# Attention loop reordered, masks by row groups, maxima split on GpSimd, setup by quads

## The reference

```python
x = x + tanh(g_xattn[0]) * L0_xattn(layernorm(x), ctx)       # 16 heads of 8, biases; context reshaped per head
x = x + tanh(g_ffn[0])   * L0_ffn(layernorm(x))              # ternary weights, quantized activations, gelu
x = x + tanh(g_xattn[1]) * L1_xattn(layernorm(x), ctx)       # one head of 128
x = x + tanh(g_ffn[1])   * L1_ffn(layernorm(x))              # as F0, gated
x = x + tanh(g_xattn[2]) * L2_xattn(layernorm(x), ctx)       # 16 query heads, one key and value head
x = x + tanh(g_ffn[2])   * L2_ffn(layernorm(x))              # switch: each row to 1 of 8 experts
x = x + tanh(g_xattn[3]) * L3_xattn(layernorm(x), ctx, mask) # 16 heads, causal, masked query rows
x = x + tanh(g_ffn[3])   * L3_ffn(layernorm(x))              # 128->512, 9 butterfly stages, gelu, 9 stages, 512->128
```

## Time and profile before

| | |
|---|---|
| median of 3 runs | 1479.29 us (1462.97 to 1483.99) |
| the profiled execution | 1479.73 us, span 1477.7 us, mean granted clock of TensorE 0.834 |
| busy PE, PEld | 1070.0 us (72%), 585.5 us (40%) |
| busy DVE, ACT, POOL | 930.5 us (63%), 683.8 us (46%), 271.2 us (18%) |
| attention of L0, first to last masked maxima operand | 104.0 to 328.7 us |
| attention of L2, the same | 618.1 to 857.8 us |
| end of routing, then the expert slots | 857.8 to 917.5, to 1028.4 us |
| attention of L3, the same | 1104.5 to 1385.5 us |

### The profile page before, as it was taken

How to read it: one execution, slowest core, us unless ns; L and a number is a source line. 1 busy time by engine, 2 the same in 40 slices (tenths; PEclk the granted TensorE clock), 3 DMA queues, 4 the chain that set the end, 5 groups by cost and what they waited for, 6 DMA issues and landing times.

```text
span 1477.7 us, 27813 instructions
## 1 busy us (share of the span) xinstructions
PE 1070.0 (72%) x8534; PEld 585.5 (40%) x8534; DVE 930.5 (63%) x2571; ACT 683.8 (46%) x1465; POOL 271.2 (18%) x398
## 2 busy tenths in 40 slices
PE   0848777775667466688988873988057888888889
PEld 0623334332345233234444441665012333333389
DVE  3824777764989899367756633777644555555444
ACT  0213555543865465457655531444023544544356
POOL 1220000000000000001222234799497000000000
PEclk9955999995669676599978865999557999999989
DMA  8270554435999100000000001222321000000001
GB/s 196 85 65 6 41 44 34 34 29 143 173 159 147 57 1 1 0 2 2 5 12 8 8 8 36 82 76 71 88 72 58 1 2 1 2 2 1 1 22 36
DMA packets 285143, 66.91 MB, mean 45 GB/s; under 512 B 206113, under 2 KB 277857, under 8 KB 285026
## 3 DMA queue, kind: packets, MB, share of 16 engines
q1 hardware_dynamic: 271968, 48.40, 22.7%
q0 software_dynamic: 4896, 14.18, 2.8%
q10 hardware_dynamic: 8162, 2.80, 0.8%
HBM read 34.80 MB, written 30.56 MB: 44 GB/s over the span
## 4 chain that ended last, share of the span: by engine, by line
PE 46%; DVE 29%; issue 13%; POOL 4%; ACT 3%; DMA 3%; ACTq 2%; DVEq 2%; another core or an unknown queue 0%; SPq 0%; POOLq 0%
PE bank L960 15%; PE bank L987 5%; DVE nmax L1371 4%; PE bank L963 3%; PE bank L953 3%; PE bank L1033 2%; PE bank L956 2%; DVE small L1545 2%; PE bank L1245 2%; PE bank L1253 2%; PE bank L971 2%; DVE o_inv L1453 2%; PE bank L1022 2%; PE bank L1072 1%; DVE q_one L1537 1%
## 5 line engine op out<-in xcount | busy, mean ns | idle before, releaser
L1371 DVE TENSOR_REDUCE nmax<-bank 128x8 f32<-128x1024 f32 x192 | 235.1, 1225 | 259.9 <-PE bank L963 254.8
L685 ACT ACTIVATE probs_space<-bank 128x1024 f32<-128x1024 f32 x192 | 196.4, 1023 | 337.7 <-PE bank L971 335.3
L960 PE MATMUL bank<-q_one,k_all 32*128 32x512 f32 x768 | 243.2, 705 | 19.0 <-DVE nmax L1371 10.6
L963 PE MATMUL bank<-k_one,q_all 32*128 32x512 f32 x768 | 248.9, 725 | 5.2 <-ACT k_one L693 3.4
L987 PE MATMUL bank<-probs_space,vals 128*32 128x128 f32 x3072 | 135.4, 298 | 0.0
L987 PEld LDWEIGHTS bank<-probs_space,vals 128*32 128x32 f32 x3072 | 78.0, 116 | 137.9 <-issue 136.9
L558 POOL TENSOR_TENSOR var_b<-stats 128x4 f32<-128x4 f32 x8 | 1.6, 203 | 706.9 <-DVE stats L1282 706.9
L960 PEld LDWEIGHTS bank<-q_one,k_all 32*128 32x128 f32 x768 | 66.6, 199 | 73.2 <-issue 72.2
L971 PE MATMUL bank<-nmax_one,ones_bf 12*128 12x512 bf16 x384 | 84.5, 412 | 0.0
L1412 DVE TENSOR_TENSOR nmax_one<-bank,max_row 128x512 bf16<-128x512 bf16 x96 | 66.3, 691 | 26.9 <-PE bank L1022 26.6
L1022 PE MATMUL bank<-ident_bf,nmax_parts 128*128 128x128 bf16 x96 | 22.7, 236 | 77.6 <-DVE nmax_parts L1399 74.4
(11 more groups left out here) (271 smaller groups left out, 2353.4 us busy)
## 6 DMA issues: line engine op xcount, KB each, us to landing
expert_rows<-zeros SPq DMA_DIRECT2D x8, 2128.5 KB, 35.0
late<-in_L_ffn_up_weights_dram POOLq DMA_DIRECT2D x9, 512.0 KB
late<-_L_ffn_down_weights_dram POOLq DMA_DIRECT2D x9, 512.0 KB
q_one<-expert_rows SPq DMA_DIRECT2D x40, 64.5 KB
x<-in_x_dram SPq DMA_DIRECT2D x4, 512.0 KB, 13.6
...
```

The source lines that it names most:

```text
L685: act.activation(probs[:, 2 * g:2 * g + 2, :, :].rearrange("k g i q -> k (g i q)"), bank_pair[1][:, :, :].rearrange("k g f -> k (g f)"), A ...
L960: pe.matmul(bank[2 + s], group(k_all, u, 2 * g + s), group(q_one, u, 2 * g + s), start=not masked, stop=False)
L963: m = pe.matmul(bank[s], group(q_all, v, 2 * f + s), group(k_one, v, 2 * f + s), start=not masked, stop=True)
L1371: dve.tensor_reduce(nmax[:, u % 2, 0, :].rearrange("q (g i) -> q g i", i=HG)[:, 2 * g:2 * g + 2, :], bank_pair[0][:, :, :].rearrange("q g ...
```

## The change

- **Attention order.** TensorE starts an iteration with the pair and the values product; the transposes of the output and of the parts follow; the output product moves behind the second pair. The wait for the masked maxima operand (`t_nm`) moves from the front of a pair to right before its matmuls against ones. VectorE does the maxima first, then the operand of line 1412.
- **Split.** In L0 and L3 the split runs on GpSimd (`split_maxima`), in L2 it stays on VectorE, interleaved with reciprocal and output. Query copies 0 and 1 go to ScalarE in L0 and L3.
- **Masks.** Per pair sixteen matmuls of 32 rows and 128 columns, each in the row group whose scores it precedes, from tables of 32-row blocks (`future_rep`, `past_rep`, `keep_rep`, `ident_blocks_bf`), which VectorE builds between F2 and L3.
- **Setup.** x and context are loaded in pieces of 1, 2, 2 and 3 quads; the norm is made per piece on GpSimd (`norm_of`). `project(c)` handles a quad: ScalarE normalizes, TensorE transposes and projects, VectorE adds biases, SyncE stores it. It is called in iterations t = c - 14 of L0, so all eight come before the pairs of quad 0; quad 0 is reloaded at t = -13. Loads of the other weights move to SyncE's queue (`later_weights()`, at t = 1).
- **Routing.** The ring of normalized rows is written by GpSimd; distances shrink, and GpSimd is one quad behind, not two.
- **F2 and butterfly.** The contraction matrix is loaded after L2; it, the bias and the mask are transposed at the front of F2. All butterfly steps move to `beside_last_attention()`: per tile of L3 a split and then three steps (four from the 55th step on).
- Several semaphores are shared under new names.

```diff
+SPLIT_BY_POOL = ("L0", "L3")
+STATS_BEFORE = {"L2": 5, "L3": 7}
+NORMS = {"L2": 4, "L3": 5}
...
+R_XT, R_HOT, R_RANK, R_ROW = 7, 10, 11, 12
...
+PROJECT = 14
+CHUNKS = ((0, 1), (1, 3), (3, 5), (5, 8))
...
+    def chunk_load(c):
+        first, last = CHUNKS[c]
+        b, columns = slice(QT * first, QT * last), slice(QT * first * P, QT * last * P)
+        sp.dma_start(x[:, columns].rearrange("p (b d) -> p b d", d=P),
+                     A["x"][b].rearrange(tok)).then_inc(S(f"chunk_in{c}"), 16)
+        if c == 0:
+            layer0_weight(2, "L0_xattn_wv")
+            layer0_weight(1, "L0_xattn_wk")
+            layer0_weight(3, "L0_xattn_wo")
+        sp.dma_start(context[:, columns].rearrange("p (b d) -> p b d", d=P),
+                     A["ctx_1024"][b].rearrange(tok)).then_inc(S(f"ctx_in_o_back{c}"), 16)
+    layer0_weight(0, "L0_xattn_wq")
     for c in range(4):
+        chunk_load(c)
...
+    def later_weights():
+        for n in range(2):
+            sp.wait_ge(S(f"q_out_slot_in{n}"), 16 * NQ // 2)
...
+            c = t + PROJECT
+            if live(c, NQ):
+                rows = slice(QT * c, QT * c + QT)
+                for n, (scratch, stage, name) in enumerate(((q_scratch, stage_q, "q_out_slot_in"),
+                                                            (v_scratch, stage_v, "st_v"))):
+                    sp.wait_ge(S("a_qv"), 2 * c + n + 1)
+                    past(sp, f"{name}{c % 2}", 16 * (c // 2))
+                    sp.dma_start(scratch[rows].rearrange("u h (r c) d -> (h r) u (c d)", r=8),
+                                 stage[:, rows, :]).then_inc(S(f"{name}{c % 2}"), 16)
+            if t == 1:
+                later_weights()
...
+    def norm_of(first, n):
+        at, mean2, diff2 = slice(first, first + n), twice_mean[:, 0:n], spread[:, 0:n]
+        link(pool.tensor_tensor(var_b[:, at], stats[:, at, 1], stats[:, at, 4], ALU.subtract), False)
+        link(pool.tensor_tensor(var_a[:, at], stats[:, at, 2], stats[:, at, 5], ALU.add), False)
...
+        link(pool.tensor_tensor(shift[:, at], mean2, var_a[:, at], ALU.mult))
+    for first, last in CHUNKS:
+        pool.wait_ge(S("stats"), QT * last)
+        norm_of(QT * first, QT * (last - first))
+        pool.sem_inc(S("a_norm"), 1)
...
+    def split_maxima(first, v):
+        done = 4 * (first + v)
+        whole, left = (nmax[:, v % 2, i, :].rearrange("q (g i) -> q g i", i=HG) for i in range(2))
+        rows = nmax_parts[:, v % 2, :].rearrange("q (g n i) -> q g n i", g=NG, i=HG)
+        pool.wait_ge(S("t_mx"), 2 * (first + v + 1))
+        past(pool, "t_mt", first + v - 1)
+        pool.tensor_copy(rows[:, :, 0, :], whole).then_inc(S("t_na"), 1)
...
+    def beside_last_attention():
         pool.wait_ge(S("w_f3"), 16 * 2)
         pool.wait_ge(S("con_T"), 1)
-        pool.wait_ge(S("wq_ready"), 5)
+        pool.wait_ge(S("B_res"), NT)
+        butterfly_weights(0)
+        butterfly_weights(1)
+        k = 0
+        for v in range(NT):
+            split_maxima(2 * NT, v)
+            for _ in range(3 if k < 6 * STAGES else 4):
+                if k < 12 * STAGES:
+                    butterfly_step(k)
+                    k += 1
+    for v in range(NT):
+        split_maxima(0, v)
...
+            norm_of(QT * c, QT)
+            past(pool, f"scattered_{c % 4}", 16 * QT * (c // 4))
+            for w in range(QT * c, QT * c + QT):
+                pool.tensor_scalar(ring[:, w % ROUTE_RING, 0:P], tile_of(x, w), rstd[:, w:w + 1], shift[:, w:w + 1],
+                                   ALU.mult, ALU.add).then_inc(S("R_xn"), 1)
...
-        for c in range(NQ + 2):
+        for c in range(NQ + 1):
             if c < NQ:
                 norm_of_quad(c)
-            if c >= 2:
-                rows_of_quad(c - 2)
-                scatter(c - 2)
+            if c >= 1:
+                rows_of_quad(c - 1)
+                scatter(c - 1)
...
-            if "F3" in phases and s_no == 0:
-                butterfly_weights(0)
-                butterfly_weights(1)
-            if "F3" in phases and s_no >= 2:
-                butterfly_step(s_no - 2)
-    if "F3" in phases:
-        pool.wait_ge(S("B_res"), NT)
-        for k in range(NS - 2, 12 * STAGES):
-            butterfly_step(k)
+    beside_last_attention()
...
         def pair_of_scores(u, g, v, f):
             if live(u):
-                pe.wait_ge(S("t_nm"), tiles + u + 1)
-                pe.wait_ge(S("t_q1"), 2 * (quads + u // QT + 1))
-                pe.wait_ge(S("t_q1_dve"), 2 * (quads + u // QT + 1))
+                pe.wait_ge(S("t_q23"), 2 * (quads + u // QT + 1))
+                pe.wait_ge(S("t_q01"), 2 * (quads + u // QT + 1))
                 past(pe, "t_ex", 2 * (tiles + u) + g)
             if live(v):
+                pe.wait_ge(S("t_qa"), quads + v // QT + 1)
                 pe.wait_ge(S("t_k1"), HG * (quads + v // QT + 1))
                 past(pe, "t_mx", 2 * (tiles + v) + (1 - f))
             if masked:
-                for s in range(2):
-                    if live(u):
-                        pe.matmul(bank[2 + s], future_bf[:, :], over_blocks(keep_diag[:, u, :], HG),
-                                  start=True, stop=False)
-                    if live(v):
-                        pe.matmul(bank[s], keep_diag[:, v, :], over_blocks(future_bf[:, :], HG),
-                                  start=True, stop=False)
+                for b in range(HG):
+                    at = slice(HR * b, HR * b + HR)
+                    for s in range(2):
+                        if live(u):
+                            rows = slice(HR * (2 * g + s), HR * (2 * g + s) + HR)
+                            pe.matmul(bank[2 + s].rearrange("k (i q) -> k i q", i=HG)[:, :, at],
+                                      future_rep[rows, b, :], over_blocks(keep_rep[rows, u, b, :], HG),
+                                      start=b == 0, stop=False)
+                        if live(v):
+                            rows = slice(HR * (2 * f + s), HR * (2 * f + s) + HR)
+                            pe.matmul(bank[s].rearrange("q (i k) -> q i k", i=HG)[:, :, at],
+                                      past_rep[rows, b, :], over_blocks(ident_blocks_bf[rows, :], HG),
+                                      start=b == 0, stop=False)
...
             if live(u):
+                pe.wait_ge(S("t_nm"), tiles + u + 1)
...
+            u, w = t - lag, t - R_XT
+            routed = layer == "L2" and live(w)
+            if not own and t == 0:
+                pe.wait_ge(S("a_qv"), 2 * NQ)
+            pair_of_scores(t, 0, t + 2, 1)
+            if live(t - 1):
+                weighted_values(t - 1, 1)
             if layer == "L2":
-                past(pe, "t_oe", tiles + min(u, NT))
-                w = t - R_LG
-                if live(w):
-                    pe.wait_ge(S("R_xe"), w + 1)
-                    past(pe, "R_cnt", (t - R_RANK + QT - 1) // QT)
...
             if live(u):
                 if own:
                     pe.wait_ge(S("t_on"), tiles + u + 1)
                 else:
-                    pe.wait_ge(S(f"L0_ob{u % 4}"), 16 * (u // 4 + 1))
+                    pe.wait_ge(S(f"ctx_in_o_back{u % 4}"), 16 * (u // 4 + 2))
                 past(pe, "t_oe", tiles + u)
                 pe.transpose(bank[7][:, 0:P], o_tok[:, u % 2, :] if own else o_back[:, u % 4, :], ident[:, :]
                              ).then_inc(S("t_ot"), 1)
+            if routed:
+                pe.wait_ge(S("R_xn"), w + 1)
+                pe.transpose(bank[7][:, 2 * P:3 * P], ring[:, w % ROUTE_RING, 0:P], ident[:, :]).then_inc(S("R_xt"), 1)
             if live(t + 1):
                 pe.wait_ge(S("t_na"), 4 * (tiles + t + 2))
                 past(pe, "t_nm", tiles + t + 1)
-                past(pe, "t_on", tiles + max(0, min(t - 1, NT)))
-                past(pe, "t_res", tiles + max(0, u))
+                past(pe, "t_on", done(t - 1))
+                past(pe, "t_res", done(u))
                 pe.transpose(bank[6][:, 3 * P:4 * P].bitcast(BF16)[:, 0:P], nmax_parts[:, (t + 1) % 2, :],
                              ident_bf[:, :]).then_inc(S("t_mt"), 1)
...
+            if live(u) or live(t - 1):
+                pe.wait_ge(S("t_nm"), done(t + 2))
+                past(pe, "t_on", done(t - 1))
+                past(pe, "t_res", done(u))
+            if live(u):
+                pe.wait_ge(S("t_oe"), tiles + u + 1)
+                pe.matmul(bank[6][:, 2 * P:3 * P], oT[:, u % 2, :], wo, start=True, stop=True
+                          ).then_inc(S("t_yp"), 1)
...
+            if live(v):
+                if layer in SPLIT_BY_POOL:
+                    past(dve, "t_na", 4 * (tiles + v - 1))
+                maxima(v, 1)
...
+            if layer not in SPLIT_BY_POOL and quad(t, 2) is not None:
+                one_head_queries(quad(t, 2), 0)
+            if layer not in SPLIT_BY_POOL and quad(t, 1) is not None:
+                one_head_queries(quad(t, 1), 1)
+            if live(v):
```

(34 more changed lines are left out.)

546 lines of the change are left out of this document (265 added, 281 removed).

## The result

The changed kernel takes **1221.47 us** (median of 4 runs, 1218.27 to 1227.54) against 1481.64 us of the kernel before in the same comparison: ratio 0.8284, 95% interval 0.8195 to 0.8372. The direction was right, and the gain of 256 us in the profiled executions (1479.7 to 1223.5; spans 1477.7 to 1221.8) is 47 us more than the 209 summed.

The account below looks back on a forecast made before the run. A chain through several engines, no engine being full, was taken to pace the attention stages (745 of 1477.7 us). Savings of 45 + 32 + 23 + 59 + 18 + 24 + 8 = 209 gave 1271 us, range 1225 to 1340.

Parts of the forecast that it names:

- The attention order: Attention loop: two halves of 1.20 + 1.23 + 0.34 (hand-over after the maximum), 5.54 us; layer 0 saves 32 us.
- The surcharge per quad: Attention loops: work done once per four tiles (projections, one-head copies) adds 0.35 us per tile, bounds 0 and 0.8.
- Layer 2: Attention of layer 2: 6.5 us per tile (bounds 6.2 and 7.2) plus 15 for low clock, 216 us, 23 less.
- The masks: Layer 3 attention: sixteen small mask matmuls take 0.45 us per pair instead of 0.95; the layer takes 222, 59 less.
- The clock: Start of each attention layer: three or four half-clock iterations cost 10, 5, 11 us; layer 2 another 10 for routing gaps.
- The butterfly and the expert stage: Butterfly moved beside layer 3: slots 2.30 us, expert stage 18 less; stretch between experts and layer 3 24 less.
- rival 1: Layer 3: GpSimd is late, a split late by one 1.6 us step in all 31 intervals: 1321 us; chance 0.10.
- The setup: Before the first masked maxima: projections end at 42 us, scores come at 57 against 104; 45 less taken (35 to 55).
- rival 2: Layer 3: the small masks save nothing, 32 us more, 1303 us; chance 0.10.
- rival 3: Layer 2 or 0: the clock stays low, 68 us more, 1339 us; chance 0.08.
- rival 4: Attention loops: the new order does not shorten them, layers 0 and 2 stay at 6.9; 1346 us; chance 0.05.
- rival 5: Layer 3: small mask matmuls do not overlap and each pays a latency, 268 us more, 1539 us; chance 0.04.

Follow-up runs that it names:

- The mirror: Kernel before the change, with only the t_nm wait moved from the front of a pair to right before the matmuls against ones: 1449.06 against 1468.30 us, ratio 0.989.

## Why the prediction was right, and where it was off

- **The attention order: right, its chain mis-sized by the hand-over.** The forecast took two halves of 1.20 + 1.23 + 0.34. The runs show 1.20 + 1.23 + 0.19, so 5.25 instead of 5.54; what differs is the one wait that the change moved from the front of a pair and that the forecast did not price. The mirror shows it in full (-0.26 per tile), its undoing in the changed kernel in good part (+0.2, and nothing in layer 2). Over the 62 intervals of layers 0 and 3, 0.29 makes 18 of the 61 us; in layer 2 the forecast did not rest on this chain.
- **The surcharge per quad** was taken as 0.35; in layer 0 the four-interval pattern 5.26, 5.25, 6.19, 5.91 has a mean of 5.65, 0.40 above the steady one. Right.
- **Layer 2** was forecast with a mean of 6.5 and 15 us for the low clock; it took 6.2 (196.0 less the first three intervals of 23.2, over 28) and 5 us, the whole surplus of 21 us. The split left on VectorE is interleaved with reciprocal and output and off the chain; the steady interval is 5.42. The 10 us for gaps around routing did not come: the granted clock is 0.95 (0.87 before).
- **The masks** were taken as 0.45 per pair between 0.24 and 0.95; they cost 0.22. The nearest row, the values product, was the wrong one to lean on; the lower bound, a quarter of the four-group time, was close. 0.23 x 2 x 31 = 14 us. Undoing them costs 41, against the 31 x 2 x 0.5 = 31 of the forecast step.
- **The clock** was forecast to be low for three or four intervals in each layer; it is for two or three (7.63, 7.97 and 7.85 at the start of layer 0, 8.25 and 8.20 in layer 3). The granted clock is 0.50 in the first 24 us of layer 0 and 0.55 in the first 17 of layer 3, then 0.98 and 1.00. These intervals cost 7 and 4 us more than the usual ones there, for 10 and 11 forecast: 10 us. With 18, 21 and 14 from the items above this is 63, against the 61 measured.
- **The butterfly and the expert stage: right**, 2.31 us per slot against 2.30, the one-column operation at 0.15, the stretch to layer 3 within 3 us. "It fits, narrowly" was right too: rival 1 did not happen (TensorE never waits for GpSimd in layer 3), and the reason given for nothing being stretched (VectorE has slack) was the weak one. VectorE's operations that read a bank are not stretched at all, nor is the statistics operation; those of the split wait for GpSimd's step, and none of these is left in layer 3.
- **The setup: the step that failed.** "Statistics of the last 12 tiles 3, their norm on GpSimd 3, 12 tiles at most 1.27 each: 42" took them to follow the data. They follow VectorE's instruction order, in which the third piece's stand behind the additions of quad 0 and the fourth's behind those of quad 2. The last twelve tiles took the 15 us forecast for them (49.96 to 65), but they began 23 us late: the projections ended at 65, not 42. What came after was right (15 us forecast, 16.4 taken).
- **The rivals** 2 to 5 are out: masks at 0.22 (2, 5), a clock of 0.92 to 0.96 (3), intervals of 5.25 and 5.62 (4).
